# Wider rows for the split values of an attention kernel, with the low values moved to column 72

## The reference

```
wp, wo = normalized weights (1536 x 512, 512 x 512)
h   = wp @ x                        per pixel; q, k, v of 8 heads
q, k = pixnorm(q) * s, pixnorm(k) * s;   v = pixnorm(v)
attn = softmax(q . k over the 1024 pixels)
res  = attn @ v;   res = wo @ res
out  = (0.7 * x + 0.3 * res) / sqrt(0.58)
```

## Time and profile before

| what | us |
|---|---|
| median of three executions | 3014.3 |
| the profiled execution, its own time | 3014.43 |
| its span (first to last instruction) | 3012.6 |
| PE busy | 2967.4 (98%) |
| PE weight loads busy | 2021.3 (67%) |
| DVE busy | 2586.9 (86%) |
| ACT busy | 2368.0 (79%) |
| POOL busy | 491.1 (16%) |

### The profile page before, as it was taken

How to read it: one execution, slowest core, us unless ns; L and a number is a source line. 1 busy time by engine, 2 the same in 40 slices (tenths; PEclk the granted TensorE clock), 3 DMA queues, 4 the chain that set the end, 5 groups by cost and what they waited for, 6 DMA issues and landing times.

```text
span 3012.6 us, 85444 instructions
## 1 busy us (share of the span) xinstructions
PE 2967.4 (98%) x36928; PEld 2021.3 (67%) x36928; DVE 2586.9 (86%) x3197; ACT 2368.0 (79%) x2993; POOL 491.1 (16%) x678
## 2 busy tenths in 40 slices
PE   6999999999999999999999999999999999999997
PEld 5766676666667666676666766667666666766664
DVE  6898898888889889898888988889888898888986
ACT  5887787877878777787777878788787787877785
POOL 0211121111211121112111121112211121111210
PEclk9999999999999999999999999999999999999999
DMA  3223324224142342433223322332322324224143
GB/s 102 52 41 69 78 51 103 54 60 93 37 103 51 65 88 40 106 58 75 65 61 85 58 75 65 72 82 51 92 60 62 87 42 102 54 61 92 33 86 92
DMA packets 459529, 211.04 MB, mean 70 GB/s; under 512 B 407952, under 2 KB 407952, under 8 KB 459152
## 3 DMA queue, kind: packets, MB, share of 16 engines
q1 hardware_dynamic: 459152, 205.58, 30.5%
HBM read 71.30 MB, written 33.55 MB: 35 GB/s over the span
## 4 chain that ended last, share of the span: by engine, by line
PE 89%; DVE 7%; issue 2%; DMA 1%; ACT 0%; POOL 0%; SPq 0%; DVEq 0%; ACTq 0%
PE ps_pv L929 23%; PE ps_score L908 21%; PE ps_dense L886 13%; PE ps_dense L890 11%; PE ps_dense L888 11%; PE ps_dense L945 4%; PE ps_dense L947 3%; PE ps_dense L946 3%; DVE probs L721 3%; DVE arena L683 1%; DVE probs L712 1%; DVE sumsq L659 0%; DMA x_res<-in_x 0%; DVE res L733 0%; PE ps_score L956 0%
## 5 line engine op out<-in xcount | busy, mean ns | idle before, releaser
L527 ACT ACTIVATE e_tile<-ps_score,shift 128x1024 f32<-128x1024 f32 x1024 | 1112.5, 1116 | 282.6 <-PE ps_score L908 273.5
L721 DVE TENSOR_TENSOR probs<-e_tile,probs 128x1024 f16<-128x1024 f32 x1024 | 1237.3, 1236 | 4.2 <-ACT probs L534 0.2
L929 PEld LDWEIGHTS ps_pv<-v_pair,probs 128*128 128x128 f16 x24576 | 782.0, 97 | 179.0 <-issue 129.6
L929 PE MATMUL ps_pv<-v_pair,probs 128*128 128x65 f16 (+1 forms) x24576 | 838.9, 193 | 10.3 <-DVE probs L721 5.7
L908 PE MATMUL ps_score<-qkT 64*128 64x512 f16 x6144 | 754.4, 378 | 8.9 <-DMA qkT<-arena 6.9
L886 PE MATMUL ps_dense<-wpT_hi,x_hi 128*128 128x512 f32 x1536 | 643.7, 419 | 2.0 <-DVE wpT_lo L792 1.8
L890 PE MATMUL ps_dense<-wpT_hi,x_lo 128*128 128x512 f32 x1536 | 603.3, 393 | 0.0
L888 PE MATMUL ps_dense<-wpT_lo,x_hi 128*128 128x512 f32 x1536 | 600.4, 391 | 0.0
L534 ACT ACTIVATE probs<-e_tile 128x1024 f16<-128x1024 f32 x512 | 543.5, 1061 | 55.1 <-PE ps_pv L929 38.9
L712 DVE CAST probs<-e_tile 128x1024 f16<-128x1024 f32 x512 | 360.3, 704 | 154.5 <-PE ps_pv L929 125.2
L908 PEld LDWEIGHTS ps_score<-qkT 64*128 64x128 f16 x6144 | 257.4, 94 | 347.1 <-issue 85.4
(11 more groups left out here) (50 smaller groups left out, 1865.5 us busy)
## 6 DMA issues: line engine op xcount, KB each, us to landing
x_raw<-in_x SPq DMA_DIRECT2D x128, 256.0 KB, 3.0
x_res<-in_x SPq DMA_DIRECT2D x128, 256.0 KB, 3.6
out<-x_res SPq DMA_DIRECT2D x128, 256.0 KB, 2.4
arena<-in_w_proj SPq DMA_DIRECT2D x24, 128.0 KB, 2.9
qkT<-arena SPq DMA_TRANSPOSE x128, 4.8
resT<-res_split SPq DMA_TRANSPOSE x128, 3.4
arena<-in_w_out SPq DMA_DIRECT2D x1, 1024.0 KB, 7.3
```

The lines of the kernel that those rows point to most:

```text
L527: act.activation(e_tile[:, t % E_BUFS, :, :], ps_score[:, t % 2, :, :], ACT.Exp, bias=shift[:, 0:1], scale=1.0 / (QK_UP * QK_UP)).then_inc ...
L721: dve.tensor_tensor(probs_of(b, t, 1), e_tile[:, t % E_BUFS, :, :], probs_of(b, t, 0), ALU.subtract).then_inc(probs_low, 1)
L929: mm = pe.matmul(ps_pv[:, h, o:o + n], probs_of(b, t, part)[:, h, queries], v[:, cols], start=(j == 0 and it == 0 and part == 0 and cols.s ...
```

## The change

The row of `v_pair` was 130 columns (260 bytes) and is 160 columns (320 bytes) now. The low values began in column 65 (byte 130 of the row) and begin in column 72 (byte 144). The columns 65 to 71 and 136 to 159 are not used. Shapes and counts of all instructions stay as they are.

Beside this, in the opening, one reduction of the first batch is placed eight ticks earlier, three weight scalings are placed 8 to 16 ticks later, and three low parts of weights 8 ticks earlier.

```diff
-FIRST_REDUCE_AT = (-3960, -3912, -3904, -3896, -3880, -3840, -3776, -3768, -3720, -3680)
+FIRST_REDUCE_AT = (-3960, -3912, -3904, -3896, -3880, -3848, -3776, -3768, -3720, -3680)
...
-W_SCALE_AT = (-4064, -4056, -4048, -4040, -3968, -3952, -3944, -3936, -3872, -3864, -3856, -3848, -3832, -3816,
+W_SCALE_AT = (-4064, -4056, -4048, -4040, -3968, -3952, -3944, -3936, -3872, -3864, -3856, -3840, -3824, -3800,
     -3792, -3784)
-W_LOW_AT = (-4024, -4016, -4008, -4000, -3824, -3808, -3800, -3760, -3744, -3736, -3728, -3672, -3664, -3656,
+W_LOW_AT = (-4024, -4016, -4008, -4000, -3832, -3816, -3808, -3760, -3744, -3736, -3728, -3672, -3664, -3656,
     -3648, -3632)
...
-        VCOLS = 2 * D + 1
         SUMS = D + 1
-        v_pair = sb("v_pair", [P, 4, NT, VCOLS + 1], F16)
+        LOW = D + 8
+        VCOLS = 2 * D + 32
+        v_pair = sb("v_pair", [P, 4, NT, VCOLS], F16)
...
-                dve.tensor_tensor(v[:, :, :, D + 1:VCOLS],
+                dve.tensor_tensor(v[:, :, :, LOW:LOW + D],
...
-                            for part, cols in ((0, slice(0, SUMS)), (0, slice(D + 1, VCOLS)), (1, slice(0, SUMS))):
+                            for part, cols in ((0, slice(0, SUMS)), (0, slice(LOW, LOW + D)), (1, slice(0, SUMS))):
```

## The result

The changed kernel takes 3002.2 us (median of 6 runs, 3001.9 to 3003.0), the kernel before 3014.5 in the same comparison (6 runs): ratio 0.9959, 95% interval 0.9946 to 0.9971. That is 12.4 us less, clear of noise. Forecast were 29.7 us less (2984.6) within 2976 to 3001. The direction was right, the size less than half, and the range missed by 1.2 us.

What follows compares the result with a forecast made beforehand. PE was taken as the bound: 3014.4 us - 37.7 for the low-value matmuls + 8.0 lost to DVE = 2984.7, by the median 2984.6; other terms zero, range 2976 to 3001.

Steps and rivals of the forecast that it cites:

- The bound: Whole kernel: PE sets the end, busy 98% of the span and 89% of the chain of waits.
- 8192 matmuls by 33.8 - 29.2 = 4.6 ns is 37.7 us: L929 on PE: each matmul on the low values loses its longer gap once they begin at byte 144.
- The lower bound: L929 triples: group means leave 1.5 to 2.4 ns over the expected cost, 12 to 20 us in all.
- The wider row: Rows of 320 bytes, 1920 bytes more of each partition: nothing seen to depend on it, counted zero.
- The loss to DVE: Where the chain runs over DVE once a batch, PE's saving is lost: 4.5 to 11.5 us over 16 batches.
- The writers: L506 on ACT and L692 on DVE, writing values into rows: neither gaps nor begin cost anything, zero.
- The opening: Moved low parts and reduction on DVE are absorbed in its idle time: zero, with 0.7 us either side.
- No change: L929: the 4.6 ns belong to weight load, even count or three accumulations; 3014.3 us, chance 10%.
- Half of it, pieces of 16 bytes: L929 reads: cost follows pieces of 16 bytes touched, nine before and eight after; 21 us stay, 2993.3, chance 4%.
- The gain eaten by half: DVE's stretch in each batch grows and eats half of PE's gain: 2995 us, chance 4%.
- The place in a block: 65-column reads: rows at multiples of 64 bytes may all begin at a bad place, 75.4 us more, 3089.7, chance 2%.
- The formula: Matmul spacing on PE: N / 2.4 + 2.5 ns, 29.2 ns at 64 columns; by it the sum stays.

Runs made afterwards that it cites:

- e8: e3 with the second and third matmul of each triple swapped: 2998.8 us, 0.9946 of before.
- e14: e5 with the low values at column 73, 2 bytes past a multiple of 16: 2992.9 us, 0.9925 of before.
- e5: e3 with all three matmuls of a triple reading 64 columns, the sum of the probabilities left out: 2981.8 us, 0.9890 of before.
- e3: Changed kernel with the four accumulators of a head in PSUM 66 columns apart in place of 65: 2998.6 us, 0.9944 of before.
- e7: e3 with the first and third matmul reading 72 columns, accumulators 72 columns apart: 3024.8 us, 1.0033 of before.
- e1: Kernel before with rows of 160 columns and the low values still at column 65 (byte 130): 3007.5 us, 0.9974 of before.
- e4: Kernel before with the changed tables of the opening alone: 3015.2 us, 1.0001 of before.
- e13: e5 with the low values at column 68 (byte 136), 8 bytes past a multiple of 16: 2982.1 us, 0.9889 of before.
- e15: e5 with all three reads beginning 8 bytes past a multiple of 16: 2983.2 us, 0.9892 of before.
- e12: e3 with the high values beginning at column 4 (byte 8), low values still at column 72: 2993.3 us, 0.9929 of before.
- e10: e3 with the high values beginning at column 6 (byte 12), low values still at column 72: 2995.1 us, 0.9936 of before.
- e16: e3 with the high values beginning at column 2 (byte 4), low values still at column 72: 2997.6 us, 0.9941 of before.
- e11: e3 with the high values beginning at column 7 (byte 14), low values still at column 72: 3008.6 us, 0.9980 of before.
- e2: Kernel before with rows of 130 columns and the low values moved to column 66 (byte 132): 3006.8 us, 0.9971 of before.

## Why the prediction was wrong

**The bound** was right: PE, in the chain with 90%.

**The failed step is "8192 matmuls by 33.8 - 29.2 = 4.6 ns is 37.7 us".** The slot measured 12.9 ns less, 13.2 us; per low-value matmul 1.6 ns. I had read the gap behind one matmul as that matmul's own cost and its neighbours' 29.1 to 29.8 as the undisturbed cost. They aren't separate: e8 moved the long gap without changing the sum, and in e14 the one dear read has its long gap behind the next matmul. After the change, the sum of a triple fell by 1.4 ns and not by 4.6, and the long gap came half as often behind the first matmul. In e5, where the 65-column reads are gone too, all of it vanished: 37.4 ns a slot, 38.3 us by the trace, 32.8 in time. That this is near the 37.7 of the forecast is chance: 12.9 of the 37.4 ns are the change's, 4.4 the accumulators' of e3, and 20.1 come with the 64-column reads, 6.7 of them as 16 columns less.

The lower bound held the result, but by luck. The runs of 96 and 48 matmuls against the 512-column matmuls left 1.5 to 2.4 ns over a triple, 12 to 20 us in all; I set it aside as "a difference of two roundings". 13.2 us lies in it. That end with 1.5 ns gave 3005.7, which I wrote down and left out of the range. Had the range held it, it would have held the result. Yet the bound took 3.1 to 3.4 ns a matmul beside its columns, of which the earlier trace rows give only the 3.4, and e5 and e7 measure 2.5. With 2.5 the triple before, 92.0 ns, stands 3.6 ns above its columns, 29 us in all, and the same argument would have forecast twice what came. Of the 3.6 ns the change took 1.4 and the accumulators of e3 another 0.7; the 1.5 left go with the 65-column reads. Neither of my two measures could tell how much of the excess was the low values'.

**The wider row, put at nothing.** The prediction saw nothing that depends on the pitch or on the 1920 bytes. e1, with that alone, has 2.1 ns a slot less and 4.1 us less on the projections, and takes 7.3 us less. So a term that was counted as zero may have more than half of the 12.4 us in time, and without it the miss would have been larger. Where the part in the projections comes from stays open.

**The loss to DVE** (4.5 to 11.5 us of 37.7, 12 to 31%) fits in size. All starts to next starts of L929 and L930 add up to 796.9 us before and 786.2 after: of 13.2 us saved in the gaps, 2.4 (18%) came back as waits. In e5, 38.3 us became 32.8 (14% lost). That DVE took them isn't shown: by the profile the waits for L721 rose by 0.5 us alone, from 5.7 to 6.2, and DVE's share of the chain fell from 7% to 6%, where it was to rise. The projections became 2.6 us shorter, scores and outputs 1.5 us longer and the rest 0.3 shorter: 12.2 us in all from PE's first start to its last, against 12.4 in time, 0.8 a batch where 1.6 to 2.1 was forecast.

**The writers** cost nothing: 682 and 637 ns, where the earlier trace rows had 686 and 639. **The opening** gave no time (e4), though the first score of the changed kernel came 1.0 us later, 0.3 more than I allowed.

**The rivals.** "No change": fell with the measurement. Its three owners of the long gap fell too, the weight load with e8, the even count and the three accumulations with e5, which has both and no long gap in its triples. "Half of it, pieces of 16 bytes", 2993.3: fell with e13 and e15. The Trainium skill (SBUF — State Buffer, Door 1: The DMA port swizzle) lets each crossing to a new line of 16 bytes pay; for TensorE's moving operand of 64 columns the runs show no such price (e13 and e15, 704.3 and 705.6 ns against 704.7). The gain eaten by half, 2995: 18% of it came back as waits. "The place in a block": 65-column reads do have better begins than byte 0 (e12 at byte 8 has 6 ns a slot less than e3), but e1, which brings all of them to byte 0 and the low ones to byte 2, took 2.1 ns less and not more. So neither its direction nor its price, 75 us, came.

**The formula** of the Trainium skill (TensorE: Matmul & The Clock Gate, Back-to-back issue gap), N / 2.4 + 2.5 ns, gives 87.5 ns for three reads of 64 columns and 94.2 for 72, 64 and 72; measured 87.6 and 94.3. For 65 columns it is too low by 0.9 to 1.6 ns a triple (e3, e10, e12, e16), by where the reads begin, and by 3.3 where they begin at byte 14 (e11).

**What stays open:** why 65 to 69 columns cost 0.6 to 1.5 ns a triple above their columns (begins at byte 14 aside) and 64 and 72 don't, what made the projections shorter, why the stall comes once in three or in six matmuls, and what in e2 makes a low read at byte 4, 8 or 12 beside 65-column reads as dear as at byte 2, when at byte 8 beside 64-column reads it is free. Six rules (L, C, U, P, R and the 8-byte one) were tried, and none holds for all 18.

## What to carry to other kernels

Don't let a row that TensorE streams begin 2 bytes past a multiple of 16; 0 and 8 bytes past were as good for 64 columns, though beside 65-column reads only a begin at a multiple of 16 is shown to gain (the changed kernel). Look at the column count as well: beyond its columns a triple with 65-column reads costs 0.8 to 1.5 ns that one of 64 alone doesn't. The kernel that puts the high values at byte 8, the low ones at byte 144 and the accumulators 66 columns apart (e12) takes 2993.3 us, 0.9929 of before, with everything computed. Count nothing as zero because no row speaks of it: the wider row alone took 7.3 us off (e1), for reasons that are in part still open. In a stream of short matmuls, take the cost from a long run divided by its count, and never from the gap behind one of them: the gap says when a delay shows, not who made it.

## What the runs showed of the hardware

- A matmul whose moving row of 64 float16 columns begins at byte 2 past a multiple of 16 costs 1.9 ns more than at byte 0 or 8 (slot 719.8 against 704.7 and 704.3 ns), at 29.2 ns each.
- A long gap doesn't name the matmul that causes it: gaps of 33 to 36 ns come once in three or six matmuls, and swapping the second and third matmul of a triple moved them and left the slot at 724.7 ns against 724.8. With the second read alone made dear (e14) they stand behind the third.
- With two of four accumulators at odd float32 columns of PSUM (65 apart), 24 matmuls cost 4.4 ns more than with all four at even ones (66 apart): 729.2 and 724.8 ns a slot.
- 65 and 66 columns in two of three reads cost the same (724.8 and 724.6 ns a slot), 68 cost 13.7 ns a slot more than 66, 69 another 5.9 (68 and 69 with accumulators 72 apart in place of 66).
- 65 columns that begin 8 bytes past a multiple of 16 take 6 ns a slot less than at 0 (718.8 and 724.8), at 14 bytes past 14 ns more (738.7).
